# An LSTM-like recurrence on 128 partitions: input gate and candidate in one 128x128 multiplication, both halves doing the same step

## What is computed

```
xi = xt @ U_i + b_i
xg = xt @ U_c + b_c
xo = xt @ U_o + b_o
def step(carry, xs):
    h, c = carry
    i_t = sigmoid(xi_t + h @ V_i)
    g_t = tanh(xg_t + h @ V_c)
    o_t = sigmoid(xo_t + h @ V_o)
    c_new = h * c + i_t * g_t
    h_new = o_t * tanh(c_new)
    return ((h_new, c_new), h_new)
```

## Time and profile before

| | us |
|---|---|
| median of the three executions | 1088.16 |
| the profiled execution | 1085.05 |
| span of its records | 1083.2 |
| recurrence, first matmul of step 0 to first of step 255 | 192.7 to 629.2 |
| busy TensorE matmul / weight load / VectorE / ScalarE / GpSimd in the whole span | 800.7 / 584.8 / 648.6 / 603.9 / 442.2 |

### The profile page before, as it was taken

The page is one execution under the profiler, slowest core; times in us unless marked ns, Lnnn a source line. Parts: engine busy times, 40 slices in busy tenths (PEclk is TensorE's granted clock), DMA queues, the critical chain, the costliest instruction groups (busy, mean ns, idle before and its releaser), DMA issues.

```text
span 1083.2 us, 18938 instructions
## 1 busy us (share of the span) xinstructions
PE 800.7 (74%) x6224; PEld 584.8 (54%) x6224; DVE 648.6 (60%) x1576; ACT 603.9 (56%) x1660; POOL 442.2 (41%) x343
## 2 busy tenths in 40 slices
PE   5787876666666666666666467877876999999996
PEld 2565664555555555555555434665753666556664
DVE  4999972355535535433333339999925766656775
ACT  2575763333335545433333326666746888878884
POOL 0688775000000000000000006788845888868885
PEclk8899987555555555555555558889986999999998
DMA  9500000000000200000000000000000010010000
GB/s 224 128 1 0 0 1 1 1 1 1 1 1 17 118 3 1 1 1 1 1 1 1 1 0 2 1 1 0 0 1 1 2 67 4 3 70 2 2 2 20
DMA packets 5852, 18.41 MB, mean 17 GB/s; under 512 B 1093, under 2 KB 2822, under 8 KB 5254
## 3 DMA queue, kind: packets, MB, share of 16 engines
q1 hardware_dynamic: 5478, 17.21, 5.5%
q10 hardware_dynamic: 288, 0.13, 0.1%
HBM read 9.47 MB, written 0.52 MB: 9 GB/s over the span
## 4 chain that ended last, share of the span: by engine, by line
POOL 35%; PE 20%; issue 19%; ACT 12%; DVE 12%; DVEq 1%; POOLq 1%; DMA 0%; SPq 0%; ACTq 0%
POOL zw L790 19%; POOL hid L754 15%; PE bank L464 9%; DVE cell L1040 5%; PE bank L466 5%; ACT tcell L696 5%; ACT scan_io L692 5%; DVE hr L1046 4%; PE bank L304 2%; PE bank L271 1%; POOL xs L747 1%; PE bank L283 1%; PE bank L337 1%; POOLq L789 1%; DVEq L1039 0%
## 5 line engine op out<-in xcount | busy, mean ns | idle before, releaser
L754 POOL TENSOR_TENSOR hid<-smat,shi 128x512 f16<-128x512 f32 x144 | 219.2, 1547 | 560.0 <-ACT smat L598 559.9
L790 POOL TENSOR_TENSOR zw<-hid,zw 128x512 f16<-128x512 f32 x176 | 204.3, 1161 | 49.9 <-ACT zw L723 33.2
L464 PE MATMUL bank<-hr,lv 64*64 64x8 f32 x512 | 96.9, 261 | 166.5 <-DVE hr L1046 166.5
L464 PEld LDWEIGHTS bank<-hr,lv 64*64 64x64 f32 x512 | 72.6, 200 | 213.1 <-DVE hr L1046 212.9
L1145 DVE SCALAR_TENSOR_TENSOR hid<-bank,wsc,st 128x512 f32<-128x512 f32 x176 | 132.0, 751 | 76.6 <-ACT st L727 70.2
L692 ACT ACTIVATE scan_io<-bank 64x16 f32<-64x16 f32 x256 | 49.2, 192 | 210.4 <-PE bank L466 210.2
L879 DVE TENSOR_TENSOR st<-tent,tentx 128x768 f32<-128x768 f32 x96 | 155.9, 1689 | 1.7
L1040 DVE TENSOR_TENSOR_SCAN cell<-scan_io 64x32 f32<-64x32 f32 x256 | 55.4, 216 | 160.2 <-ACT scan_io L692 160.1
L507 PE MATMUL bank<-st,wh 128*128 128x512 f16 x352 | 136.9, 389 | 11.9 <-POOL st L783 5.4
L727 ACT ACTIVATE st<-bank,wsc 128x512 f32<-128x512 f32 x176 | 121.0, 688 | 36.3 <-PE bank L508 18.7
L508 PE MATMUL bank<-st,wl 128*128 128x512 f16 x352 | 136.8, 389 | 0.0
(11 more groups left out here) (149 smaller groups left out, 1274.1 us busy)
## 6 DMA issues: line engine op xcount, KB each, us to landing
w13s<-w SPq DMA_DIRECT2D x8, 704.0 KB, 16.6
w2f<-w SPq DMA_DIRECT2D x4, 384.0 KB, 26.6
w13s<-wh SPq DMA_DIRECT2D x2, 704.0 KB, 3.4
w13s<-wl SPq DMA_DIRECT2D x2, 704.0 KB, 4.6
wh<-w13s SPq DMA_DIRECT2D x2, 704.0 KB, 4.3
wl<-w13s SPq DMA_DIRECT2D x2, 704.0 KB, 5.5
w2f<-w2p SPq DMA_DIRECT2D x2, 384.0 KB, 5.1
w2p<-w2f SPq DMA_DIRECT2D x2, 384.0 KB, 5.2
```

The costliest lines, as they stand in the source:

```text
L464: nc.tensor.matmul(both[:, 0, t, :], lv[:, C:2 * C], prev, start=False, stop=True, skip_group_check=True)
L754: nc.gpsimd.tensor_tensor(slo[:, place(p, g), :, :], smat[:, g % RING, :, :], shi[:, place(p, g), :, :], ALU.subtract).then_inc(s(c + "s_l ...
L790: nc.gpsimd.tensor_tensor(hl[:, u % MR, :], hid[:, u % MR, :], hh[:, u % MR, :], ALU.subtract)\
```

## The change

The state is now on all 128 partitions. `hr` holds for each step a 128 x 2 x 8 block: partitions 0 to 63 hold h in the columns k = 0 and zero in the columns k = 1, partitions 64 to 127 the other way round (block-diagonal). The weights `lv` hold in slot 0 the input gate's on rows 0 to 63 and the candidate's on rows 64 to 127, twice side by side, so one multiplication of 128x128 by 16 columns gives the input gate in its columns k = 0 and the candidate in its columns k = 1, on both halves of the partitions. Slot 1 holds the output gate's block-diagonally, in a second multiplication of 128x128 by 16. Its bias is -80 where the block is to be empty, so that a true Sigmoid gives 0 there, and the product with tanh(c) writes h and the zeros at once. h is no longer doubled. The cell and its tanh are computed twice, once on each half, and h times c by two instructions of 64 partitions each, one for each half. `gates_x` has eleven pieces of 128 columns of weights, one of them a bias by 256 columns (k = 6). The 3 loads become 18, placed after the router's and behind a wait for three fills by POOL. `hr` and `hup` lie in the memory of `smat`, which the convolutions use. `FILL`, which was 0, goes.

```diff
+SHUT = -80.0
...
-FILL = 0
...
-        lu = sb("lu", [P, 2, 192])
-        lv = sb("lv", [C, 192])
-        lb = sb("lb", [1, 192])
+        lu = sb("lu", [P, 2, 4, P])
+        lv = sb("lv", [P, 2, P])
+        lb = sb("lb", [2, 3, P])
         ones = sb("ones", [1, 128])
-        hr = sb("hr", [C, 2 * W, B])
-        scan_io = sb("scan_io", [C, 2, B, 4])
-        cell = sb("cell", [C, B, 4])
-        tcell = sb("tcell", [C, B])
-        tog = sb("tog", [C, B])
-        hup = sb("hup", [P, 2, BQ, W])
+        scan_io = sb("scan_io", [P, 2, B, 4])
+        cell = sb("cell", [P, B, 4])
+        tcell = sb("tcell", [P, B])
+        og = sb("og", [P, 2, B])
...
+        hr = spare[:, 0:4 * W * B].rearrange("p (n k b) -> p n k b", k=2, b=B)
+        hup = spare[:, 512:512 + 2 * BQ * W].rearrange("p (q b t) -> p q b t", q=2, b=BQ)
...
-            sp.dma_start(lu[:, :, :], lstm_u).then_inc(s("ld_lstm"), 16)
-            sp.dma_start(lv[:, :], lstm_v).then_inc(s("ld_lstm"), 16)
-            sp.dma_start(lb[:, :], lstm_b).then_inc(s("ld_lstm"), 16)
             sp.dma_start(rw[:, :], router).then_inc(s("ld_late"), 16)
+            sp.wait_ge(s("l_blank"), 3)
+            cand, inp, outp = slice(0, C), slice(C, 2 * C), slice(2 * C, 3 * C)
+            for k in range(2):
+                own = slice(k * C, k * C + C)
+                sp.dma_start(lu[:, :, 0, own], lstm_u[:, :, inp]).then_inc(s("ld_lstm"), 16)
+                sp.dma_start(lu[:, :, 1, own], lstm_u[:, :, cand]).then_inc(s("ld_lstm"), 16)
+                sp.dma_start(lu[:, :, 2 + k, own], lstm_u[:, :, outp]).then_inc(s("ld_lstm"), 16)
+                sp.dma_start(lv[0:C, 0, own], lstm_v[:, inp]).then_inc(s("ld_lstm"), 16)
+                sp.dma_start(lv[C:2 * C, 0, own], lstm_v[:, cand]).then_inc(s("ld_lstm"), 16)
+                sp.dma_start(lv[own, 1, own], lstm_v[:, outp]).then_inc(s("ld_lstm"), 16)
+                sp.dma_start(lb[0:1, 0, own], lstm_b[:, inp]).then_inc(s("ld_lstm"), 16)
+                sp.dma_start(lb[0:1, 1, own], lstm_b[:, cand]).then_inc(s("ld_lstm"), 16)
+                sp.dma_start(lb[k:k + 1, 2, own], lstm_b[:, outp]).then_inc(s("ld_lstm"), 16)
             for e in range(PAIRS):
                 for hf in range(2):
...
@@ -422,24 +432,33 @@
 
 
             norm(1, [("c0_res", 1 + BQ)])
-            pe.wait_ge(s("ld_lstm"), 16 * 3)
+            pe.wait_ge(s("ld_lstm"), 16 * 18)
             pe.wait_ge(s("n1_xn"), 2)
-            pe.wait_ge(s("l_scaled"), 4)
+            pe.wait_ge(s("l_scaled"), 3)
             pe.wait_ge(s("l_init"), 4)
 
             def gates_x(r, k):
 
                 q = r % 2
-                gate, part = k // 3, k % 3
-                lo = (C, 0, 2 * C)[gate]
-                bk, col = (bank[2 + q], 0) if gate == 2 else (bank[q], gate * 128)
-                if part == 0:
-                    nc.tensor.matmul(bk[0:C, col:col + 128], lb[:, lo:lo + C], ones[:, :],
-                                     start=(gate != 1), stop=False, skip_group_check=True)
+                rhs = xn[:, :].rearrange("p (b t) -> p b t", b=BQ)[:, :, r * W:r * W + W]
+                if k < 6:
+                    gate, part = k // 3, k % 3
+                    bk, col = bank[q], gate * 128
+                    if part == 0:
+                        nc.tensor.matmul(bk[:, col:col + 128], lb[0:1, gate, :], ones[:, :],
+                                         start=(gate == 0), stop=False, skip_group_check=True)
+                    else:
+                        hf = part - 1
+                        nc.tensor.matmul(bk[:, col + hf * C:col + hf * C + C], lu[:, hf, gate, :], rhs,
+                                         start=False, stop=False, skip_group_check=True)
+                elif k == 6:
+                    nc.tensor.matmul(bank[2 + q][:, 0:256], lb[:, 2, :],
+                                     ident[0:2, 0:2].unsqueeze(2).broadcast_to([2, 2, 128]),
+                                     start=True, stop=False, skip_group_check=True)
                 else:
-                    hf = part - 1
-                    rhs = xn[:, :].rearrange("p (b t) -> p b t", b=BQ)[:, :, r * W:r * W + W]
-                    nc.tensor.matmul(bk[0:C, col + hf * C:col + hf * C + C], lu[:, hf, lo:lo + C], rhs,
+                    copy, hf = (k - 7) // 2, (k - 7) % 2
+                    col = copy * 128 + hf * C
+                    nc.tensor.matmul(bank[2 + q][:, col:col + C], lu[:, hf, 2 + copy, :], rhs,
                                      start=False, stop=False, skip_group_check=True)
 
             def largest_weights():
@@ -453,29 +472,24 @@
                 nc.tensor.matmul(bank[5][:, 0:2], ones[:, :], wpow[:, 2, :], start=True, stop=True)\
                     .then_inc(s("w_bc"), 1)
 
-            for k in range(9):
+            for k in range(11):
                 gates_x(0, k)
             for n in range(STEPS):
                 r, t = n // W, n % W
                 pe.wait_ge(s("l_h"), n + 1)
-                prev = hr[:, (n - 1) % (2 * W), :]
-                both = bank[r % 2][0:C, 0:256].rearrange("p (k b t) -> p k t b", k=2, t=W)
-                go = bank[2 + r % 2][0:C, 0:128].rearrange("p (b t) -> p t b", t=W)[:, t, :]
-                nc.tensor.matmul(both[:, 0, t, :], lv[:, C:2 * C], prev, start=False, stop=True,
-                                 skip_group_check=True)
-                nc.tensor.matmul(both[:, 1, t, :], lv[:, 0:C], prev, start=False, stop=True,
+                prev = hr[:, (n - 1) % (2 * W), :, :].rearrange("p k b -> p (k b)")
+                both = bank[r % 2][:, 0:256].rearrange("p (kb t) -> p t kb", t=W)
+                go = bank[2 + r % 2][:, 0:256].rearrange("p (kb t) -> p t kb", t=W)
+                nc.tensor.matmul(both[:, t, :], lv[:, 0, :], prev, start=False, stop=True,
                                  skip_group_check=True).then_inc(s("l_gi"), 1)
-                nc.tensor.matmul(go, lv[:, 2 * C:3 * C], prev, start=False, stop=True,
+                nc.tensor.matmul(go[:, t, :], lv[:, 1, :], prev, start=False, stop=True,
                                  skip_group_check=True).then_inc(s("l_o"), 1)
                 if n == POWER + 2:
                     largest_weights()
                 elif n == POWER + 7:
                     spread_scales()
-                if 3 <= t < 12 and r + 1 < H:
+                if 3 <= t < 14 and r + 1 < H:
                     gates_x(r + 1, t - 3)
-                for _ in range(FILL):
-                    nc.tensor.matmul(bank[7][:, :], samp[0][:, 0, 0:128], samp[0][:, 0, 0:512],
-                                     start=True, stop=True)
 
 
...
@@ -679,19 +693,20 @@
 
                 if r >= 2:
                     act.wait_ge(s("l_res"), r - 1)
-                nc.scalar.activation(hup[C * hf:C * hf + C, r % 2, :, :],
-                                     hr[:, r % 2 * W:r % 2 * W + W, BQ * hf:BQ * hf + BQ].rearrange("p t b -> p b t"),
-                                     ACT.Copy, scale=0.5).then_inc(s("l_up"), 1)
+                own = slice(C * hf, C * hf + C)
+                nc.scalar.copy(hup[own, r % 2, :, :],
+                               hr[own, r % 2 * W:r % 2 * W + W, hf, BQ * hf:BQ * hf + BQ].rearrange("p t b -> p b t"))\
+                    .then_inc(s("l_up"), 1)
 
             act.wait_ge(s("l_init"), 4)
             for n in range(STEPS):
                 r, t = n // W, n % W
-                both = bank[r % 2][0:C, 0:256].rearrange("p (k b t) -> p k t b", k=2, t=W)[:, :, t, :]
-                go = bank[2 + r % 2][0:C, 0:128].rearrange("p (b t) -> p t b", t=W)[:, t, :]
+                both = bank[r % 2][:, 0:256].rearrange("p (k b t) -> p k t b", k=2, t=W)[:, :, t, :]
+                go = bank[2 + r % 2][:, 0:256].rearrange("p (k b t) -> p k t b", k=2, t=W)[:, :, t, :]
                 act.wait_ge(s("l_gi"), n + 1)
                 nc.scalar.activation(scan_io[:, :, :, 2], both, ACT.Tanh).then_inc(s("l_act"), 1)
                 act.wait_ge(s("l_o"), n + 1)
-                nc.scalar.activation(tog[:, :], go, ACT.Tanh).then_inc(s("l_oact"), 1)
+                nc.scalar.activation(og[:, :, :], go, ACT.Sigmoid).then_inc(s("l_oact"), 1)
                 act.wait_ge(s("l_c"), n + 1)
                 nc.scalar.activation(tcell[:, :], cell[:, :, 3], ACT.Tanh, scale=0.5).then_inc(s("l_tc"), 1)
...
             nc.gpsimd.memset(epsc[:, 1:2], 1e-5).then_inc(s("zero"), 1)
+            nc.gpsimd.memset(lu[:, :, 2:4, :], 0.0).then_inc(s("l_blank"), 1)
+            nc.gpsimd.memset(lv[:, 1, :], 0.0).then_inc(s("l_blank"), 1)
...
             conv(0)
-            gp.wait_ge(s("ld_lstm"), 48)
-            for part, factor in ((lu[:, :, C:3 * C], 0.5), (lb[:, C:3 * C], 0.5),
-                                 (lv[:, 0:C], 0.5), (lv[:, C:3 * C], 0.25)):
-                nc.gpsimd.tensor_scalar(part, part, factor, None, ALU.mult).then_inc(s("l_scaled"), 1)
+            gp.wait_ge(s("ld_lstm"), 16 * 18)
```

(14 more changed lines are left out.)

7 lines of the change are left out of this document (5 added, 2 removed).

## The result

The kernel after takes 1109.24 us (median of four executions, 1107.93 to 1109.35) against 1087.91 of the kernel before (the three executions above and a fourth of 1081.16). The two medians give a ratio of 1.0196; the estimate over the executions is 1.0212, 95% interval 1.0188 to 1.0235. The profiled execution is 1107.93 us with a span of 1106.1, 22.9 more than before. The forecast was 1098, slower with 72%: the sign and the chain of causes were right, the size was half of what came, since the cost of a step and that of the wide bias were put too low.

The account below looks back on a forecast made before the run. The recurrence was taken as a chain of waits with no engine full. Terms 5.1 + 1.0 + 2.1 + 1.8 = +10 us on 1088.2 gave 1098 us; range to hold 8 in 10: 1064 to 1125.

Parts of the forecast that it names:

- 0.00 + 0.01 + 0.01 = +0.02, times 255: +5.1 us: Recurrence step: multiplication +0.00, output gate +0.01, h with 16 elements for 8 +0.01 us; over 255 steps +5.1 us.
- I take +0.00: Input gate and candidate: one 128-column multiplication is over after 0.60 us, where the old two were; bounds -0.22 to +0.08.
- rival 1: Wide load costs half as much, 0.11 us for a pair; no late piece; 1066 us; 8%.
- The output gate: Its activation runs 1.07 to 1.26 us, overlapping the tanh of the cell by 0.09; +0.01 a step, 0 to +0.09.
- the scan keeps its 32 elements on twice the partitions: VectorE's scan in each step: same elements on twice the partitions, with no cost added to the step.
- The piece by 256 needs 0.88 and is off at 1.84: 256-column bias piece within the steps: 0.12 us late in each of 15 rows, +1.8 us.
- The pieces before step 0: Eleven pieces for nine ahead of the recurrence: 5.8 us, +2.1 us; bounds 0 and +2.5.
- VectorE, nothing: Second product h times c runs beside the multiplications in idle VectorE time, at most 0.17 us; no cost at this step length.
- idle VectorE of 0.25 or more before every scan: Sign of the forecast: VectorE keeps at least 0.25 us idle before each scan, the margin for the second product.
- The table: True Sigmoid beside Tanh on ScalarE: one more table load of 1.283 us in step 0, 0.3 hidden, +1.0 us.
- Rival 4: ScalarE's tables alternate, two loads of 1.283 us in each step on the chain: 657 us more, 1755 us; 3%.
- Rival 3: Clock rises since each matmul fills the array; multiplication over after about 0.37 us; 1040 us; 4%.

Follow-up runs that it names:

- narrow_load: Kernel after with both multiplications of a step loading 64 of their 128 columns of weights (results not the reference's): 1055.60 us, ratio 0.9741.
- fill3_after: Kernel after with three dummy float16 multiplications behind each step's work on TensorE: 1095.51 us, no ratio given.
- warm_before: Kernel before with dummy multiplications: seven in the first two steps of every fourth row, three in steps with a piece, four in others: 1040.42 us, ratio 0.9604.
- wide_partitions: Kernel before, TensorE untouched, with every step operation on ScalarE and VectorE on 128 partitions instead of 64: 1091.93 us, ratio 1.0066.
- one_product: Kernel after with one product h times c instead of two (results not the reference's): 1108.22 us, ratio 1.0206 to the kernel before.
- split_bias: Kernel after with the 256-column bias made in two pieces of 128 columns in two steps: 1107.79 us, ratio 1.0210 to the kernel before.
- stacked: Kernel before with input gate over candidate in one 128x64 weight tile, block-diagonal h written twice by VectorE: 1087.27 us, ratio 1.0010.
- stacked_pool: The version stacked, with GpSimd writing the upper block of h beside VectorE and a true Sigmoid: 1076.31 us, ratio 0.9915 to the kernel before.
- fill3_before: Kernel before with three dummy multiplications per step, as in fill3_after: 1159.16 us, no ratio given.
- warm runs: Denser dummies (seven, three or four a step) on the kernel after with split bias, 1050.69 us, and the kernel before, 1040.42; on stacked_pool, 1050.72.

## Why the prediction was half right

The step that failed is the sum per step, "0.00 + 0.01 + 0.01 = +0.02, times 255: +5.1 us": it measured +0.052, 13.2 us. That is 8.1 of the 12.9 us between the forecast of +10 and the 22.9 of the profiles. The second is the wide bias within the steps, 1.8 us in the sum and 5.4 measured. The mechanism was right, these two terms were too small:

- **"I take +0.00" for the multiplication**: right within 0.01. 0.61 against 0.60, and narrow_load shows that it is the load's width. The trace's 0.49 us for a pair by line 453 was 0.50 for line 483. The Trainium skill's rule (TensorE: Matmul & The Clock Gate, "LDWEIGHTS (loading the stationary operand)") would have had 0.11 us for a pair's additional columns; narrow_load gives 0.21 at 1.2 GHz, and 0.11 is what rows show at 2.4 GHz (0.30 in fill3_after, 0.19 in warm_before). So this case's trace agrees at 2.4 GHz and doesn't at the clock of this stage, and rival 1 falls.
- **The output gate**: right. The tanh of the cell starts at 1.20 directly behind the scan, the Sigmoid at 1.07 as forecast, and narrowing its load gains nothing in a plain step. In 12 steps the overlap of 0.09 us on which the term rests was not there, 0.9 us in all; the sum had 0.01 a step, 2.6 us, for this.
- **The step, "+0.02"**: this is the step that cost the most. The term that was put at nothing without a reason is the one dismissed in half a sentence, "the scan keeps its 32 elements on twice the partitions". Twice the partitions cost 7 to 10 ns in three operations on the chain (the fourth, the tanh of the cell, 1) and some 0.03 a step (wide_partitions, 7.2 us in 255 steps). Of the rest, 0.01 is the multiplication, and 0.007 the columns of h, for which the sum had 0.01.
- **"The piece by 256 needs 0.88 and is off at 1.84"**: this failed by the largest factor, 0.36 us a row for 0.12 (5.4 us for 1.8). The piece started at 0.96 as forecast, but took 1.15, so the step took 2.11. The pieces of 128 columns were off in time, as forecast. The length had come from line 304, whose loads are 27 columns wide, and that of the 128-column pieces from lines 437 and 442, 64 wide: narrow rows for wide pieces, right after the width of the load had been found to count. For the bias of 128 columns the traces bear this out: from its start to that of the next piece it takes 0.61 us in the kernel before (190.22 to 190.83) and 0.72 after (189.12 to 189.84). For the one of 256 columns no run separates the load from the columns that move. The pieces before step 0, sized by line 283 with its wide loads, came to 2.7 us for 2.1, and there the rows were nearer.
- **VectorE, nothing**: right in the plain step (one_product), though two products occupy it for 0.40 us and not 0.34. The margin behind it was misread: 0.25 us was not the shortest idle time before a scan. In the kernel before, 0.07 stands in front of the scan at 305.86, and in the kernel after VectorE isn't idle at all before five scans. The sign "idle VectorE of 0.25 or more before every scan" did not come; only one of those scans is late by more than 0.02 us, by 0.15, so that little hung on it was luck.
- **The table**: right. One more load of 1.283 us, in step 0, 1.0 us; none afterwards. Rival 4 falls: after that one load Tanh and Sigmoid run side by side, which agrees with what the Trainium skill says (ScalarE: Activation LUTs, "Table sets: the hidden batching unit"). Of the drain of 1.38 us that the Trainium skill gives (the same page, "What ACT_TABLE_LOAD costs") nothing shows: the load begins 0.02 us after the tanh before it has ended, and the Sigmoid 0.01 us after the load.
- **The clock**: right, 0.50 throughout with TensorE busier than before. Rival 3's price was near for the multiplication (0.40 for 0.37 at the full clock); no run of the change alone reached that clock.
- **18 loads, the wait on SP, `smat`**: nothing that can be told from the scatter; the stretches outside the recurrence are 0.6 us shorter in the two profiled executions, and they differ by 8.6 us between the kernel after and split_bias. No run tests these alone.

With the sizes put right, 13.2 + 5.4 + 0.9 + 2.7 + 1.0, the sum is 23.2 us and the forecast would have been 1111.

## What to carry to other kernels

In a chain of small float32 multiplications count columns of weights, not instructions: here, merging two 64-column multiplications into one of 128 columns saved nothing, and stacking them over the rows saved 0.21 us of TensorE's time, of which the step kept only what the wider h left (nothing in stacked, 0.05 in stacked_pool). Whoever widens an operation has to size everything that rides along (the pieces in the gaps, the partitions) by rows of the new width. And when a stage runs at half the clock, that is the first thing to look at: dummy multiplications that hold the granted clock at 1.00 gave 4% here, where the rearrangement took 2%.

## What the runs showed that was not expected

- Operations of VectorE on 128 partitions take 8 to 10 ns longer than on 64 with the same elements per partition (scan 225 for 216, product 167 for 157); on ScalarE the tanh of the gates takes 199 for 192, and the tanh of the cell the same 216 for 215.
- Two operations of VectorE on the two halves of the partitions don't overlap: 0.35 us for the two writes of h in stacked, 0.37 for the two products in the kernel after. A reduction that follows a single product starts 0.09 us after the start of it, while it still runs.
- With three dummies a step the granted clock is 1.00 for stretches and 0.50 for others in one execution, and four executions of fill3_before spread over 1085 to 1253 us. TensorE wasn't idle where it was low: matmuls were in flight for 50.00 of 50 us at 0.50 and for 46.34 at 1.00. Why the clock stays low there is open; with the denser dummies of the warm runs it stayed at 1.00.
- GpSimd, idle otherwise, can join a chain of 0.2 us operations: 0.20 us for a 64 x 8 product, 0.04 more than VectorE, a start 0.04 later, and 0.06 more until TensorE starts.
